# Two causal attentions of a decoder: V products of four heads side by side, masks on GpSimd, a third slot of stacks, loops unrolled

## The reference

```
scores = q @ k.T * scale          # scale is 1/4 in layer 0, 1 in layer 1
scores = where(key after query, -inf, scores)
out    = softmax(scores) @ v
```

## Time and profile before

| what | us |
|---|---|
| median of 3 runs | 5155.61 |
| lowest and highest run | 5147.95, 5156.69 |
| the profiled execution, its own time | 5149.44 |
| its span in the trace | 5147.7 |
| TensorE busy | 4235.4 (82%) |
| VectorE busy | 3352.6 (65%) |
| GpSimd busy | 2149.4 (42%) |
| ScalarE busy | 2014.9 (39%) |

### The profile page before, as it was taken

One profiled execution on the slowest core, in us unless ns is written; L12 is line 12 of the kernel. 1 busy time (PEld: TensorE's weight loads), 2 busy tenths in 40 slices (PEclk: granted clock), 3 DMA queues, 4 the chain that ended last, 5 costly groups with the idle time before them and its releaser, 6 DMA issues. The chain is left out here.

```text
span 5147.7 us, 54277 instructions
## 1 busy us (share of the span) xinstructions
PE 4235.4 (82%) x16800; PEld 2327.3 (45%) x16800; DVE 3352.6 (65%) x5430; ACT 2014.9 (39%) x3247; POOL 2149.4 (42%) x1631
## 2 busy tenths in 40 slices
PE   5888888888888888598477787999967788979898
PEld 1233333333333333244222225888833344668788
DVE  4999999999999999935654444444355444143433
ACT  4666666666666665233123332111112333323100
POOL 6888888888888888300200001444320000000320
PEclk8999999999999999899778898999987899976899
DMA  2222222222222222100322211000061212000000
GB/s 79 63 65 77 64 72 64 78 64 72 65 78 63 71 65 67 46 18 1 93 24 29 29 15 41 26 26 25 1 166 25 42 28 34 9 15 0 25 17 29
DMA packets 223212, 240.72 MB, mean 47 GB/s; under 512 B 100481, under 2 KB 131516, under 8 KB 222716
## 3 DMA queue, kind: packets, MB, share of 16 engines
q1 hardware_dynamic: 222972, 237.82, 17.6%
HBM read 209.58 MB, written 25.69 MB: 46 GB/s over the span
## 5 line engine op out<-in xcount | busy, mean ns | idle before, releaser
L473 POOL TENSOR_TENSOR arena<-arena 128x512 f32<-128x512 f32 x1024 | 1280.0, 1271 | 289.2 <-DVE arena L760 282.1
L760 DVE TENSOR_TENSOR_SCAN arena<-psum,arena 128x512 f32<-128x512 f32 x1024 | 1275.6, 1246 | 91.1 <-POOL arena L473 50.8
L865 PE MATMUL psum<-arena,base 128*128 128x512 f32 x2048 | 1112.4, 643 | 265.5 <-DVE arena L735 260.1
L638 ACT ACTIVATE psum<-arena 128x512 f32<-128x512 f32 x1024 | 704.5, 689 | 773.0 <-DVE arena L760 769.5
L865 PEld LDWEIGHTS psum<-arena,base 128*128 128x128 f32 x2048 | 357.3, 196 | 906.5 <-DVE arena L735 751.2
L1117 DVE TENSOR_REDUCE arena<-psum 128x1 f32<-128x512 f32 (+3 forms) x768 | 412.8, 556 | 419.7 <-PE psum L1183 332.8
L735 DVE TENSOR_TENSOR arena<-arena,psum 128x512 f32<-128x512 f32 x1024 | 678.4, 663 | 0.0
L224 POOL TENSOR_TENSOR rounded<-arena,rounded 128x512 fp32r<-128x512 f32 (+2 forms) x181 | 315.8, 1751 | 826.4 <-DVE rounded L220 826.4
L230 PE MATMUL psum<-rounded 128*128 128x256 f32 (+1 forms) x1728 | 561.0, 325 | 38.0 <-DVE arena L1646 17.7
L231 PE MATMUL psum<-rounded 128*128 128x256 f32 (+1 forms) x1728 | 560.3, 324 | 0.0
L232 PE MATMUL psum<-rounded 128*128 128x256 f32 (+1 forms) x1728 | 559.6, 324 | 0.0
(11 more groups left out here) (280 smaller groups left out, 5877.7 us busy)
## 6 DMA issues: line engine op xcount, KB each, us to landing
arena<-mb_b_rows SPq DMA_DIRECT2D x512, 256.0 KB, 3.1
arena<-L_ffn_w SPq DMA_DIRECT2D x34, 512.0 KB, 4.6
arena<-f_parts SPq DMA_DIRECT2D x96, 128.0 KB, 6.0
arena<-l_parts SPq DMA_DIRECT2D x96, 128.0 KB, 5.8
l_v<-arena SPq DMA_DIRECT2D x16, 512.0 KB, 4.4
arena<-l_v SPq DMA_DIRECT2D x32, 256.0 KB, 7.5
f_parts<-arena SPq DMA_DIRECT2D x24, 256.0 KB, 2.4
l_parts<-arena SPq DMA_DIRECT2D x24, 256.0 KB, 2.3
```

The source lines that it names most:

```text
L473: eng.tensor_tensor(drive[:, u % RD, :], dtu[:, g % 2, m, :], b_sb[:, v % RB, :], ALU.mult)\
L638: eng.activation(ps[:, DECAY + u % 2, :], dt[:, g % 2, m, :], ACT.Exp, scale=a_neg[:, g // 4 % 2, m, n:n + 1]).then_inc(decay_ready, 1)
L760: eng.tensor_tensor_scan(h[:, u % RH, :], ps[:, DECAY + u % 2, :], drive[:, u % RD, :], first, ALU.mult, ALU.add).then_inc(scanned, 1)
L865: mm = eng.matmul(ps[:, Y + u % 2, :], sh.ident, hc[:, u % RW, :], start=False, stop=n == NS - 1)
```

## The change

It changes `causal_attention` for both attentions, in five ways.

1. **Products in fours.** In the narrow attention the products of units u-1 and u are made together, when u is odd: two heads of one unit and two of the next, at the same block of keys, one behind the other with no score among them. `between(2)` follows them. In the wide attention they stay as they are.
2. **Masks on GpSimd.** The matmuls with `mask_k` go. In their place GpSimd waits for the exponential of a unit with a diagonal block (16 of 24 units, `cut`) and writes zeroes into the corner of both blocks, 128 x 2 x 128 float32, in place. `products` of such a unit waits for `masked`, not `exped`.
3. **A third slot of stacks.** Slots of `qs` and `ks` become 3. The third uses the staging buffers `st` and `rest` of `write_parts`, free once the parts are sent. Before the first group, stacks 0, 1 and 2 are loaded. When group i is done, SP issues V of i+2 and then the stacks of i+3.
4. **Unrolled.** All 8 groups are straight code on every engine, with constant addresses and waits.
5. **Constants.** The one memset of rows 96 to 98 becomes one per slot; that of the third slot is made on GpSimd after the parts are sent, and TensorE waits for it ahead of a group. `mask_k` isn't built.

The core of the diff:

```diff
+    SLOTS = 3
-    qs = sh.take(None, 2 * G * S // 2).bitcast(BF16).rearrange("p (r h s) -> p r h s", r=2, h=G)
-    ks = sh.take(None, 2 * G * S // 2).bitcast(BF16).rearrange("p (r h s) -> p r h s", r=2, h=G)
+    qs, ks = ([sh.take(None, G * S // 2).bitcast(BF16).rearrange("p (h s) -> p h s", h=G) for _ in range(SLOTS - 1)] + [late]
+              for late in (part.rearrange("p r s -> p (r s)").bitcast(BF16).rearrange("p (h s) -> p h s", h=G) for part in staged))
...
+    cut = [u for u in range(U2) if units2[u][1][0][1] >= 4 * units2[u][0]]
...
-        load_stacks(0, 0)
-        load_stacks(1, 1)
+        for i in range(SLOTS):
+            load_stacks(i)
         v_wait(eng)
...
-        def body(i, r, more):
-            if more:
-                rows(i + 1, 1 - r)
-            if not isinstance(i, int):
-                eng.wait_ge(s["av_done"], (i + 1) * U2)
-                load(i + 2, r)
-
-        loop(eng, body)
+        for i in range(GROUPS):
+            if i + 1 < GROUPS:
+                rows(i + 1)
+            if i + 2 < GROUPS:
+                eng.wait_ge(s["av_done"], (i + 1) * U2)
+                load_v(i + 2)
+            if i + SLOTS < GROUPS:
+                load_stacks(i + SLOTS)
...
+    def masks(eng):
+        for slot in sent:
+            eng.wait_ge(*slot)
+        eng.memset(ks[SLOTS - 1][STACK:STACK + PARTS], -1.0).then_inc(s["init"], 1)
+        eng.wait_ge(s["init"], 6)
+        for i in range(GROUPS):
+            for u in cut:
+                eng.wait_ge(s["exped"], i * (2 * U2) + 2 * u + 2)
+                corner = ex[:, u % RE, :, 0:P]
+                eng.affine_select(out=corner, in_=corner, compare_op=ALU.is_ge, fill=0.0, base=0,
+                                  pattern=[[0, 2], [1, P]], channel_multiplier=-1).then_inc(s["masked"], 1)
...
-        def products(i, r, u, between):
-            qc, blocks, o = units2[u]
-            eng.wait_ge(s["exped"], i * (2 * U2) + 2 * u + 2)
+        def products(i, u, between):
+            first_unit = u - 1 if packed else u
+            qc, _, o = units2[u]
+            if u in cut:
+                eng.wait_ge(s["masked"], i * len(cut) + cut.index(u) + 1)
+            else:
+                eng.wait_ge(s["exped"], i * (2 * U2) + 2 * u + 2)
...
+            for n in range(first_unit, u + 1):
+                for k, (h, kt) in enumerate(units2[n][1]):
+                    first, w = span(qc, kt)
+                    rows = slice(32 * h, 32 * h + 32) if packed else slice(0, VW)
+                    mm = eng.matmul(ps[rows, ACC + o % 2, first:BANK], v[:, i % 2, kt, h, :], ex[:, n % RE, k, 0:w],
+                                    start=kt == 0, stop=kt == 4 * qc + 3)
+                    if k == 0 and between and not packed:
+                        between(2)
+            mm.then_inc(s["av_done"], u - first_unit + 1)
+            if between and packed:
+                between(2)
...
-                    diagonal = kt >= 4 * qc
-                    mm = eng.matmul(ps[:, bank + k, 0:w], ks[0:STACK + PARTS, r, h, kt * P:(kt + 1) * P],
-                                    qs[0:STACK + PARTS, r, h, qc * BANK + first:(qc + 1) * BANK],
-                                    start=True, stop=not diagonal)
-                    if diagonal:
-                        mm = eng.matmul(ps[:, bank + k, 0:P], sh.ident_bf, sh.masks.mask_k, start=False, stop=True)
+                    mm = eng.matmul(ps[:, bank + k, 0:w], ks[i % SLOTS][0:STACK + PARTS, h, kt * P:(kt + 1) * P],
+                                    qs[i % SLOTS][0:STACK + PARTS, h, qc * BANK + first:(qc + 1) * BANK],
+                                    start=True, stop=True)
...
-                if u >= LAG:
-                    products(i, r, u - LAG, between)
+                if u >= LAG and (not packed or u % 2):
+                    products(i, u - LAG, between)
```

More of the change, by code:

```diff
@@ L1100, in exponentials @@
                     take_output(i, done)
-                if more and u == TURN + 1:
+                if i + 1 < GROUPS and u == TURN + 1:
                     take_rows(eng, i + 1)
@@ L1108, in scalar @@
         take_rows(eng, 0)
-        loop(eng, exponentials)
+        for i in range(GROUPS):
+            exponentials(i)
     def vector(eng):
@@ L1163, in body, with score @@
                 output(i, o)
-        loop(eng, body)
     def tensor(eng):
-        def score(i, r, u):
+        def score(i, u):
             h, t, kc = UNITS[u]
@@ L1193, in turn_max @@
             mm.then_inc(s["mt_done"], 1)
-        def products(i, r, u, between):
-            qc, blocks, o = units2[u]
-            eng.wait_ge(s["exped"], i * (2 * U2) + 2 * u + 2)
-            if u == 0 or units2[u - 1][2] != o:
-                eng.wait_ge(s["scaled"], 4 + i * (4 * OUTS) + 4 * max(o - 1, 0))
-            for k, (h, kt) in enumerate(blocks):
-                first, w = span(qc, kt)
-                rows = slice(32 * h, 32 * h + 32) if packed else slice(0, VW)
-                mm = eng.matmul(ps[rows, ACC + o % 2, first:BANK], v[:, r, kt, h, :], ex[:, u % RE, k, 0:w],
-                                start=kt == 0, stop=kt == 4 * qc + 3)
-                if k == 0 and between:
-                    between(2)
-            mm.then_inc(s["av_done"], 1)
+        def products(i, u, between):
[5 more added lines that the diff above has]
+                eng.wait_ge(s["exped"], i * (2 * U2) + 2 * u + 2)
+            if first_unit == 0 or units2[first_unit - 1][2] != o:
+                eng.wait_ge(s["scaled"], 4 + i * (4 * OUTS) + 4 * max(o - 1, 0))
+            for n in range(first_unit, u + 1):
[9 more added lines that the diff above has]
+                between(2)
         def turn_output(i, o):
@@ L1217, in tensor @@
         for u in range(U1):
-            score(0, 0, u)
+            score(0, u)
         turn_max(0)
-        def body(i, r, more):
+        for i in range(GROUPS):
+            more = i + 1 < GROUPS
             lo = 0
             eng.wait_ge(s["rows_in"], (i + 1) * (16 * G))
-            eng.wait_ge(v_in[r], (i - r) * (v_load.count // 2) + v_load.count)
+            eng.wait_ge(s["init"], 6)
+            eng.wait_ge(v_in[i % 2], (i // 2 + 1) * v_load.count)
             for u, (qc, blocks, o) in enumerate(units2):
@@ L1397, in pool @@
         wp["pool"](eng)
+        att["masks"](eng)
     def scalar(eng):
```

97 lines of the change are left out of this document (43 added, 54 removed).

## The result

| | median us | lowest and highest | the profiled execution's span |
|---|---|---|---|
| before | 5155.1 | 5147.95, 5156.69 | 5147.7 |
| changed | 4914.25 | 4910.76, 4926.2 | 4910.2 |

The ratio is 0.954 with a 95% interval of 0.9521 to 0.9558: 241 us less by the medians, 237.5 by the two profiled spans. The forecast was 4900 in 4862 to 4960. It was 14 us too low.

A forecast was written before the change was run, and what follows sets the result against it. A group was taken as one exposed stack load, then TensorE. Narrow attention 167.5 us plus wide 90 gave 257.5 off 5149.4: 4892, by the median 4898, said as 4900; range 4862 to 4960, its own 4862 to 4925.

The forecast's parts named there:

- Products in fours: Narrow attention: four heads side by side cost one product, 18.5 us less TensorE a group, 9.2 less in the last.
- The slack: Narrow steady groups: VectorE's maxima bind next, with TensorE at 29 us; groups fall from 68.2 to 43 us, 151 in six.
- 35.1 from the start to the turn, 7.4 to the next group: Narrow group: 33.5 as in the prologue, 1.1 output, 0.5 first K·Q; then the unchanged row chain; sum 42.5 us.
- rival A: The clock sags: narrow attention at about 0.75, groups of 50 us, 50 us more in all, 4950 us; chance 15%.
- TensorE idle in some 3 us: Narrow group end: of the unchanged 7.4 us from turn to next group, TensorE idles some 3 us, waiting for rows.
- The last narrow group: Last narrow group: from 31.7 us to ScalarE's 19.5 plus hand-overs, start and end, 26.5 us; a gain of 5.
- Masks: Both attentions: 1.9 us of identity products a group leave TensorE; waits for GpSimd's select priced at 0.5 us a narrow group.
- Third slot: Stacks load a whole group before need against 12 us of transfer; gain inside the narrow 43 us, 11.5 a wide group.
- Wide groups: Wide attention: TensorE stays the bound, steady groups from 72.4 to 56.0 us at a clock near 1.00, 98 us in six.
- 72.4 less 11.5, 3.0 and 1.9: Wide steady group: 72.4 us less stack waits 11.5, slow restart 3.0 and masks 1.9, giving 56.0.
- The start of the wide attention: V stores queue behind one more slot of stacks: about 12 us longer, bounds 6.4 and 13; VectorE's wait 23.7 to 36.
- Unrolling: Loops of both attentions as straight code: priced at nothing, bounds -5 and +10 us.

The follow-up runs named there:

- the experiment: The changed kernel with the diagonal masks as identity products on TensorE again and no selects on GpSimd: 4915.2 us, 0.954 of before.
- pairs: The changed kernel with narrow products made for each unit as an undivided pair of heads, no four side by side: 4923.7 us, 0.956 of before.
- the two kernels with everything that pays: The changed kernel with one stack ahead of V and 8 idle products a group, 4867.3 us; the same with idle products around the prologues too, 4858.6 us.

## Why the prediction was right, and where not

**Products in fours: right.** The price of a quad was taken as that of one product, 0.98 us at 512 columns, and x8 blocks show it (0.99 us to the next instruction's start). The Trainium skill (TensorE: Matmul & The Clock Gate, Part 3) has 3.07x for four tiles in row groups and 2.38x for three in column groups; the trace has four for the price of one in these float32 products, so the 1.28 us worked out from it is not what happens here.

**The slack: right.** The steady group was put at 43 us, VectorE's chain binding, and the mean of six is 43.0. This is right by two errors that cancel. The step "35.1 from the start to the turn, 7.4 to the next group" is 34.3 and 6.7 where the clock is at 1.00, that is 41.0, 2 us less than forecast with its 0.5 for the masks. And in half of the groups the clock costs 3.9 us, which the forecast gave to rival A alone (15%, at 50 us a group). What came is a weaker form of it: 0.88, not 0.75. The forecast's argument against A, that no level is lost inside busy stretches, was about a kernel with TensorE full; it didn't hold for one with TensorE at 33.5 of 40.9 us.

**"TensorE idle in some 3 us" for the rows: wrong in place.** It waits 0.53 us for them. The tail's idle time, forecast as some 3 us, is there (1.10 + 0.94 + 0.19 + 0.17 + 0.72 + 0.53 = 3.65 us), but in six pieces, of which the rows' is one; most of it waits for VectorE's parts of the maxima and for ScalarE. I had counted only TensorE's work in the tail and not that its K·Q products there wait for exponentials.

**The last narrow group: undersized gain.** 23.3 us against 26.5. ScalarE is busy 18.5 of it, so that the hand-overs, start and end that I gave 7 us are 4.8.

**Masks: right in the wide attention, too high.** 1.9 us a group were priced, the experiment shows 1.4. In the narrow one half a microsecond of hand-overs was priced and 0.4 us of gain is seen at equal clock. The select's 0.47 us by the line between two rows was 0.407. The Trainium skill (GPSIMD Engine Reference, § 3.1) puts the best case of a tight loop at some 1.8 cycles an element, and the shortest loop bodies at 1.03. By an estimate from the first figure, at the page's 1.2 GHz, 128 elements more would be 0.19 us, by the second 0.11. The rows have 0.292 us for 128 elements (bfloat16) and 0.407 for 256 (float32), 0.115 more, so nearer the second; which of the two a select is, no run here shows.

**Third slot: right.** Its absence costs 135 us. In its trace, which is 8 above the median, the 12 groups are 157 longer, 11 to 17 each, and the start of the wide attention is 8 shorter.

**Wide groups: the term that was oversized.** The median missed by 14 us, the profiled spans by 20 (257 forecast, 237.6 measured), and 9.5 of the 20 are here. "72.4 less 11.5, 3.0 and 1.9" began with one group that took 72.4 where the mean of six was 72.0: 2 us in six groups. The steady wide group at full clock is 56.7, not 56.0: 4 us in six, 3 of them because the masks give 0.5 less a group. And the clock was taken as 1.00, where two of six groups had 0.97: 3.4 us.

**The start of the wide attention: right in kind, somewhat too high.** 12 us were priced, and 11.0 came between these two traces. But VectorE's wait for the stores rose from 23.7 to 30.5 us, not to 36. And over all traces the stretch is 744 to 747 us in three kernels with two stacks ahead of V and 749 to 757 in seven with three: 9 us by the means. With one stack ahead it is 729 to 738.

**Unrolling: right**, nothing.

The rest of the miss of the spans, 12.5 us, is in stretches that the diff doesn't touch and of which the longest varies by 8 us between traces of equal code. The narrow attention, 3 us better than forecast, makes up for a part. That its steady groups came out at 43.0 was luck in part: in another trace with the same code for them the six took 264.5 us, 44.1 each.

## What to carry to other kernels

Column groups pay in full only if all products of a quad stand side by side and the engine that feeds them isn't next in line: pairs had brought all but 3 us of a group, and VectorE took the rest. When TensorE stops being full, its clock becomes part of the bill: work taken off it (masks, products) may come back as a lower granted clock, and products that nobody reads, placed in its waits, cost nothing that could be seen here and held the clock. When a slot is added, look at what stands behind its first loads in the queue.

## What was not expected of the hardware

TensorE fell to its lower level behind group ends at which no wait was longer than 1.10 us. The end of the second group of the changed kernel, which fell, in TensorE's timeline:

```profile
...
2697.19 0.61 PE L1190 MATMUL psum<-base,arena 128*12 128x128 bf16 x8 [1.10 <-DVE arena L1133]
...
2703.89 1.03 PE L1247 MATMUL psum<-arena 99*128 99x512 bf16 x2 [0.53 <-DMA arena<-arena]
...
```

and the granted clock over the most of the second group up to its end, and over the start of the third:

```profile
...
2671.00:2704.00 33.00, 26.30 (x189) 9.38 (x186) 21.80 (x49) 16.15 (x22) 4.34 (x11) 0.99 0.09 11
2704.00:2712.00 8.00, 7.63 (x34) 3.10 (x33) 3.49 (x12) 3.67 (x4) 1.62 (x4) 0.50 0.97 134
...
```

The same two waits, 1.10 and 0.53 us, and the same four between them as at the end of the group shown further up, which kept its clock; here the first product of the next group takes 1.03 us in place of 0.60, and the granted clock goes from 0.99 to 0.50, its lower level of 1.2 GHz. Four groups of 44.8 us stand at 0.88; between the levels that is some 10.7 us of each at the lower one (0.12 x 44.8 / 0.5). Equal ends come out both ways, then: no single wait decides it, and what does is left open. One thing that differs is what went before: the second group had begun at the lower level, and the sixth hadn't. Once it had passed one boundary without falling it stayed at 1.00 for the rest, in this trace from the sixth group on. That isn't a rule: with the masks on TensorE groups at 1.00 were followed by one at 0.92, and in the two kernels with everything that pays the last group, which has no idle products, stands at 0.93 behind groups at 1.00. With 8 idle products of 0.22 us a group, 1.7 us of 41, it stayed up from the third group on, and in the two later kernels from the second.
